# A fused normalise, gate, attention and expert layer: first tile's statistics read from PSUM, its first projection begun with the high parts, the output weights' low parts made earlier

## The chip, the cores and the metric

The kernel runs on one core of one Trainium2 chip. The metric is the device time of one execution in microseconds (us), the median of several runs.

## What is computed

One layer on 8 images of 512 channels by 256 positions, in float32. Cut to what matters:

```
x = x + gate(group_norm(x))                    # per channel a factor from mean, max, std and the MEDIAN of all of them
t = tokens(x)                                  # 8 batches of 256 tokens, 512 wide
t = t + attention(layer_norm(t), w_q, w_k, w_v, w_o)     # 16 heads of 32, tanh softcap, causal mask
t = t + shared_mlp(layer_norm(t)) + top2_of_8_experts(layer_norm(t))
```

layer_norm is (v - mean) / sqrt(var + eps) over the 512 channels of a token.

## The kernel before, in words

Every engine has its own instruction list, written out by hand, and they meet through semaphores only. Names of engines in the profile: PE is TensorE, DVE is VectorE, ACT is ScalarE, POOL is GpSimd, SP issues loads and stores.

**High and low parts.** A float32 matmul operand is split into a high part (rounded by a copy to the type fp32r) and a low part (the operand minus the high part). A product is then three matmuls: high by high, and the two mixed ones. `triple` (line 1566) issues these three for each of the 4 blocks of 128 channels. For the attention weights the split is made in 12 pieces: ACT makes the high piece m (`high_piece`, line 714, writes w_h), POOL the low piece m (`low_piece`, line 534, writes w_l). Pieces 0 to 3 are w_q and w_k (1024 wide each), 4 to 7 are w_v and 8 to 11 are w_o (512 wide each). For the tokens, ACT makes xt_h (`xt_high`, line 743) and DVE xt_l (`xt_low`, line 1188), each in two halves of 256 channels.

**The order of the work.** First the statistics of x and a search for the median in 8 rounds (DVE line 1046 and ACT count half of the values each, PE sums over partitions). In each round ACT also makes one high piece (pieces 4 to 11). Then the lead, on one tile of 256 tokens, and after it steps of attention, one for each batch, in which PE runs the heads of one batch, the projections of the next and the output projection of the one before, all interleaved. The shared MLP and the experts follow.

**The lead** (batch 0) on the engines, in its order:

- DVE `affine(0)` (line 1150) applies the channel factors into `front`.
- PE `y_transposes` (line 1624) turns `front` to tokens, into the PSUM banks YT0 and YT1, 128 tokens each.
- ACT `tokens` (line 737) copies both banks to the SBUF tile T.
- DVE `first_norm` waits until both banks are free again, reads T for the statistics (`tile_stats`, line 1158), joins them (`tile_variance`, lines 1165 and 1167); POOL `rstd_of` (line 549) makes the reciprocal root; DVE `normalised` (line 1173) writes the normalised tile, two instructions, to `front`.
- PE `front_transposes` (line 1635) turns that back to channels, into the banks XN0 and XN1; ACT `xt_high` and DVE `xt_low` split it.
- PE `front_split` waits until XN0 and XN1 are free, that is until both halves of xt_l are made, and then runs the four projections Q0, K0, Q1, K1 (`heads_projection`), 24 matmuls of 256 columns each. Each writes two halves of a bank, 12 matmuls a half.

PE fills two gaps of the lead with dummy matmuls on the identity (`keep_busy`, line 1574; each appears as two passes in the trace). Three PSUM banks (PS5 to PS7, `ring_bank`) are used in turn by all these items; `filled` and `emptied` give the semaphore and the count that say that an item's bank is full or free again (ring_full0 to 2, ring_free0 to 2).

**The first attention step** (batch 0) on PE: scores of head pairs 0 and 1, V's projection, the transposes of the next tile, scores of pairs 2 and 3, then `head_values(0)`, the products of the masked probabilities with V (line 1686). It waits for POOL's masks of pairs 0 and 1 (line 558), for which ACT's exponentials (line 761) must be done, and for both copies of V (ACT line 750). POOL's list here is: low pieces 0 to 7, the root of batch 0, the root of batch 1, low pieces 8 to 11, then the masks of the first step.

Of the kernel before, what the change touches and what calls it, by code (L numbers as in the profile page):

```python
# [17 lines left out]
B, C, S = 8, 512, 256  # L18
# [3 lines left out]
P = 128  # L22
CB = C // P
TT = S // P
# [48 lines left out]
def ring(part, item, b):  # L73

    n = 0
    for name, (steps, items) in PARTS.items():
        if name == part:
            break
        n += steps * len(items)
    n += items.index(item)  # L80
    return n % RING, n // RING + ((b - 1) * (len(items) // RING) if part == "mid" else 0)
# [27 lines left out]
def layer_kernel(nc, x, params, wqkvo, gate, ws, wgu, wd, out):  # L109
    ctx = ExitStack()  # L110
    with ctx:

        def sb(name, shape, dt=fp32, scope=ctx):
            return scope.enter_context(nc.sbuf_tensor(name, shape, dt))
# [42 lines left out]
        w_h = sb("w_h", [P, 4, CB * C], fp32r, scope)  # L157
        w_l = sb("w_l", [P, 4, CB * C], fp32r, scope)
# [24 lines left out]
        bn6 = sb("bn6", [P, TT, 6], fp32, scope)  # L183
# [16 lines left out]
        xt_h = sb("xt_h", [P, CB, S], fp32r, scope)  # L200
        xt_l = sb("xt_l", [P, CB, S], fp32r, scope)
        front = sb("front", [P, CB * S], fp32, scope)
# [104 lines left out]
        score_bank, od_bank, ring_bank = PS[0:4], PS[4], PS[5:8]  # L307
# [7 lines left out]
        def sem(name):  # L315
            return ctx.enter_context(nc.semaphore(name))
# [9 lines left out]
        dve_step, pool_step, act_step = sem("dve_step"), sem("pool_step"), sem("act_step")  # L326
        chmean_ready, grpmean_ready, chvar_ready, grpvar_ready = (
            sem("chmean_ready"), sem("grpmean_ready"), sem("chvar_ready"), sem("grpvar_ready"))
        act_sums = sem("act_sums")
        partial_full, partial_ready = sem("partial_full"), sem("partial_ready")  # L330
        var_ready, root_ready = sem("var_ready"), sem("root_ready")
        u_ready, every_ready, spread_full, uT_full = sem("u_ready"), sem("every_ready"), sem("spread_full"), sem("uT_full")
# [5 lines left out]
        var1_ready, rstd1_ready, var2_ready, rstd2_ready = (  # L338
            sem("var1_ready"), sem("rstd1_ready"), sem("var2_ready"), sem("rstd2_ready"))
        xn_ready, xt_h_done, x2_ready = sem("xn_ready"), sem("xt_h_done"), sem("x2_ready")  # L340
# [49 lines left out]
        def tile_at(b, tt):  # L390

            return at(T, b)[:, tt * C:(tt + 1) * C]

        def filled(part, item, s):

            k, used = ring(part, item, s)
            return ring_full[k], used + 1

        def emptied(part, item, s):

            k, used = ring(part, item, s)
            return ring_free[k], used + 1
# [3 lines left out]
        QK_PIECES, V_PIECES, W_PIECES = 4, 8, 12  # L406

        def piece_of(m, attn):


            if m < QK_PIECES:
                return attn[:, m // 2, 1024 * (m % 2):1024 * (m % 2 + 1)]
            j, k = divmod(m - QK_PIECES, 4)
            return attn[:, 2 + j, 512 * k:512 * (k + 1)]
# [97 lines left out]
        def _(pool):  # L512
# [19 lines left out]
            def low_piece(m):  # L532
                pool.wait_ge(whi_done, m + 1)
                pool.tensor_tensor(piece_of(m, w_l), piece_of(m, w_in), piece_of(m, w_h).bitcast(fp32),
                                   ALU.subtract).then_inc(wlo_done, 1)
# [5 lines left out]


            pool.wait_ge(spread_full, 1)
            for m in range(V_PIECES):
                low_piece(m)

            def rstd_of(var_ready, rstd_ready, b):
                pool.wait_ge(var_ready, b + 1)
                pool.tensor_tensor(rstd[:, :], var_eps[:, :], powers[:, 0:TT], ALU.pow).then_inc(rstd_ready, 1)
# [46 lines left out]
            def step(b, has_next):  # L596
                summed = not (isinstance(b, int) and b == 0)
                for p in range(4):
                    mask(b, p, summed)
                if not (isinstance(b, int) and b == 0):  # L600
                    rstd_of(var2_ready, rstd2_ready, b - 1)
                att_low(b, 0)
                mask(b, 4, summed)
                mask(b, 5, summed)
                att_low(b, 1)
                mask(b, 6, summed)
                mask(b, 7, summed)
                att_low(b, 2)
                att_low(b, 3)
                if has_next:  # L610
                    shared_low(b)
                    rstd_of(var1_ready, rstd1_ready, b + 2)

            rstd_of(var1_ready, rstd1_ready, 0)
            rstd_of(var1_ready, rstd1_ready, 1)
            for m in range(V_PIECES, W_PIECES):
                low_piece(m)
            step(0, True)
            with pool.Fori(1, B - 2) as b:
                step(b, True)  # L620
# [69 lines left out]
        def _(act):  # L690
# [41 lines left out]
            def tokens(part, b, s):  # L732

                for tt in range(TT):
                    act.wait_ge(*filled(part, f"YT{tt}", s))
                    k, _ = ring(part, f"YT{tt}", s)
                    act.activation(tile_at(b, tt), ring_bank[k], ACT.Copy).then_inc(ring_free[k], 1)

# [198 lines left out]
        def _(dve):  # L937
# [207 lines left out]
            def affine(b):  # L1145

                xb = at(T, b).rearrange("p (k s) -> p k s", k=CB)
                ab, bb = coefA[:, bass.ds(b * CB, CB)], coefB[:, bass.ds(b * CB, CB)]
                for k in range(CB):
                    ins = dve.tensor_scalar(front[:, k * S:(k + 1) * S], xb[:, k, :], ab[:, k:k + 1], bb[:, k:k + 1],  # L1150
                                            ALU.mult, ALU.add)
                ins.then_inc(y_ready, 1)

            def tile_stats(b):

                stand_alone(dve)
                for tt in range(TT):
                    step_of(dve.bn_stats(bn6[:, tt, :], tile_at(b, tt)))

            def tile_variance(var_ready):  # L1160

                dve.wait_ge(dve_step, n.value())
                stand_alone(dve)
                for tt in range(TT):
                    step_of(dve.bn_aggr(mean_var[:, tt, :], bn6[:, tt, :]))
                dve.wait_ge(dve_step, n.value())
                dve.tensor_scalar(var_eps[:, :], mean_var[:, :, 1], EPS, None, ALU.add).then_inc(var_ready, 1)

            def normalised(dst, b, rstd_ready):

                dve.wait_ge(rstd_ready, b + 1)
                for tt in range(TT):
                    ins = dve.tensor_scalar(dst[:, tt * C:(tt + 1) * C], tile_at(b, tt), mean_var[:, tt, 0:1],
                                            rstd[:, tt:tt + 1], ALU.subtract, ALU.mult)
                return ins

            def first_norm(part, b, s):
                for tt in range(TT):
                    dve.wait_ge(*emptied(part, f"YT{tt}", s))
                tile_stats(b)  # L1180
                tile_variance(var1_ready)
                normalised(front, b, rstd1_ready).then_inc(xn_ready, 1)
# [130 lines left out]
                gate_top("last", b - 1, b)  # L1313

            affine(0)
            first_norm("lead", 0, 0)
            xt_low("front", 0, 0)
            affine(1)
            for item in ("Q0", "K0", "Q1", "K1"):
# [241 lines left out]
        def _(pe):  # L1561
            def triple(out, parts, lhs, rhs):

                products = [(k, a, b) for k in parts for a, b in ((0, 0), (0, 1), (1, 0))]
                for m, (k, a, b) in enumerate(products):
                    ins = pe.matmul(out, lhs(k, a), rhs(k, b), start=m == 0, stop=m == len(products) - 1)  # L1566
                return ins
# [44 lines left out]
            def begin(part, item, s):  # L1612

                k, used = ring(part, item, s)
                if not (isinstance(used, int) and used == 0):
                    pe.wait_ge(ring_free[k], used)
                return ring_bank[k], ring_full[k]
# [21 lines left out]
            def wslice(t, j, k, lo_, hi_):  # L1639
                return t[:, j, k * C + lo_:k * C + hi_]  # L1640
# [5 lines left out]
            def heads_projection(part, item, s):  # L1646
# [7 lines left out]
                                 lambda k, a: (xt_h, xt_l)[a][:, k, :])  # L1654
                ins.then_inc(full, 1)

            def values_projection(part, s, tt):
                bank, full = begin(part, f"V{tt}", s)
                triple(bank, range(CB), lambda k, a: (xt_h, xt_l)[a][:, k, tt * P:(tt + 1) * P],
                       lambda k, a: wslice((w_h, w_l)[a], 2, k, 0, C)).then_inc(full, 1)  # L1660
# [72 lines left out]
            def front_transposes(part, b, s):  # L1733
                pe.wait_ge(xn_ready, b + 1)
                transposes(part, "XN", front, s)

            def front_split(part, s):
                pe.wait_ge(*emptied(part, "XN0", s))
                pe.wait_ge(*emptied(part, "XN1", s))
# [91 lines left out]
            y_transposes("lead", 0, 0)  # L1831
            keep_busy(16)
            front_transposes("front", 0, 0)
            front_split("front", 0)
            pe.wait_ge(wlo_done, QK_PIECES)
            for item in ("Q0", "K0", "Q1", "K1"):
                heads_projection("front", item, 0)
            y_transposes("front", 1, 0)

# [172 lines left out]
```

## Time and profile before

| | |
|---|---|
| median of 3 runs | 718.38 us (717.37 to 720.6) |
| profiled execution | 718.36 us |
| its span | 716.6 us |
| PE busy | 649.3 us (91%) |
| DVE busy | 443.4 us (62%) |
| ACT busy | 335.8 us (47%) |
| POOL busy | 317.5 us (44%) |

The span is from the first to the last instruction of the profiled execution; its own time is what the runs measure. Busy shares are averages over stages with different limits, so what a change in one stage is worth is read from that stage's waits. In the rows below a line number is that of the kernel before.

### The profile page before, as it was taken

What the parts mean: (1) busy time and instruction counts of PE and PEld (TensorE: products, weight loads), DVE (VectorE), ACT (ScalarE), POOL (GpSimd) and SP (SyncE); (2) the same over time, 40 slices, a digit from 0 to 9 for tenths busy, and PEclk for the clock granted to TensorE, in tenths of its full rate; (3) what the DMA queues carried; (4) which work ended last, traced back from release to release, by engine and by line L of the source; (5) the groups of instructions that cost most, each with busy time, mean ns of one, the idle gap of its engine ahead of it and who ended that gap; (6) DMA issues with size and microseconds to landing.
All of it is one profiled execution on the core that took longest, in us unless ns stands there. A gap on an engine that the chain in (4) does not pass through costs nothing.

```text
span 716.6 us, 14422 instructions
## 1 busy us (share of the span) xinstructions
PE 649.3 (91%) x5030; PEld 553.2 (77%) x5031; DVE 443.4 (62%) x974; ACT 335.8 (47%) x616; POOL 317.5 (44%) x377
## 2 busy tenths in 40 slices
PE   1417989999999999999999999999899999999991
PEld 1407878888888888887789899999677877778771
DVE  7875454757575757573646995223676767667761
ACT  7641364646464646465523123434444454444540
POOL 1340343646464646462421115856345455454534
PEclk9758999999999999999999999999999999999996
DMA  9800000101010101020226323452865555556543
GB/s 307 340 0 1 1 2 1 60 1 59 0 59 0 59 0 59 1 90 1 90 76 240 116 91 113 130 176 70 299 115 96 112 98 107 105 100 111 99 70 44
DMA packets 24787, 62.62 MB, mean 87 GB/s; under 512 B 3056, under 2 KB 7920, under 8 KB 23216
## 3 DMA queue, kind: packets, MB, share of 16 engines
q1 hardware_dynamic: 14912, 41.69, 16.3%
q0 software_dynamic: 9168, 20.45, 15.7%
q8 instruction: 21, 0.34, 0.2%
q10 hardware_dynamic: 672, 0.03, 0.1%
q14 instruction: 14, 0.11, 0.0%
HBM read 39.09 MB, written 23.07 MB: 87 GB/s over the span
## 4 chain that ended last, share of the span: by engine, by line
PE 53%; DMA 27%; DVE 10%; issue 4%; POOL 3%; ACT 1%; DVEq 1%; SPq 0%; POOLq 0%; ACTq 0%
DMA out_tokens<-yo,dest 24%; PE PS L1566 21%; PE scores L1566 12%; PE scores L1858 5%; PE PS L1686 4%; PE scores L1670 3%; PE PS L1635 2%; PE PS L1693 1%; DMA out_tokens<-T 1%; DVE rden L1203 1%; DMA T<-in_x 1%; DVE front L1046 1%; POOL out_tokens L668 1%; PE PS L1624 1%; DVE front L1150 1%
## 5 line engine op out<-in xcount | busy, mean ns | idle before, releaser
L1566 PE MATMUL scores<-xb,sw_h 128*128 128x256 f32 x512 | 94.6, 285 | 0.0
L659 POOL DMA_INDIRECT out_tokens<-yo,dest x36 | 57.1, 1586 | 79.6 <-DMA out_tokens<-yo,dest 77.3
L1566 PEld LDWEIGHTS scores<-xb,sw_h 128*128 128x128 f32 x512 | 81.2, 192 | 2.2 <-ACT probs L757 0.4
L1566 PE MATMUL PS<-xt_h,w_h 128*128 128x256 f32 x256 | 74.5, 291 | 1.6 <-DVE xt_l L1188 1.6
L1566 PE MATMUL scores<-xb,sw_l 128*128 128x256 f32 x256 | 72.5, 283 | 0.0
L1566 PE MATMUL PS<-xt_l,w_h 128*128 128x256 f32 x256 | 72.4, 283 | 0.0
L1566 PE MATMUL PS<-xt_h,w_l 128*128 128x256 f32 x256 | 72.3, 283 | 0.0
L558 POOL TENSOR_SCALAR_AFFINE_SELECT probs<-probs 128x256 f32<-128x256 f32 x128 | 50.4, 418 | 45.6 <-ACT probs L761 45.4
L1566 PE MATMUL scores<-wgu_h,xgT_h 128*128 x156 | 65.0, 417 | 2.1 <-DVE xgT_l L1528 2.1
L1203 DVE RECIPROCAL rden<-PS 128x256 f32<-128x256 f32 x32 | 56.1, 1753 | 13.5 <-PE PS L1686 11.8
L577 POOL TENSOR_TENSOR hl<-hf,hh 128x256 fp32r<-128x256 f32 x32 | 28.5, 890 | 76.3 <-ACT hh L839 76.3
L1566 PE MATMUL scores<-wgu_h,xgT_l 128*128 x156 | 61.1, 391 | 0.0
L907 ACT ACTIVATE wdt_h<-wd_sb 128x512 fp32r x76 | 43.9, 624 | 36.4 <-PE scores L1566 36.4
L1566 PE MATMUL scores<-wgu_l,xgT_h 128*128 x156 | 60.9, 390 | 0.0
L757 ACT ACTIVATE probs<-scores 128x768 f32<-128x768 f32 x64 | 51.3, 802 | 11.2 <-PE scores L1670 11.1
L761 ACT ACTIVATE probs<-probs 128x768 f32<-128x768 f32 x64 | 54.1, 846 | 2.0
L1523 DVE TENSOR_TENSOR wdt_l<-wd_sb,wdt_h 128x512 fp32r<-128x512 f32 x76 | 49.1, 688 | 9.3 <-ACT wdt_h L907 7.6
L1566 PEld LDWEIGHTS PS<-xt_h,w_h 128*128 128x128 f32 x256 | 49.0, 191 | 4.8 <-issue 3.0
L571 POOL TENSOR_TENSOR att_l<-att,att_h 128x256 fp32r<-128x256 f32 x32 | 23.8, 744 | 63.8 <-ACT att_h L765 63.7
L1566 PEld LDWEIGHTS scores<-xb,sw_l 128*128 128x128 f32 x256 | 49.1, 192 | 0.0
L1566 PEld LDWEIGHTS PS<-xt_l,w_h 128*128 128x128 f32 x256 | 49.0, 192 | 0.0
L1566 PEld LDWEIGHTS PS<-xt_h,w_l 128*128 128x128 f32 x256 | 49.0, 192 | 0.0
(304 smaller groups left out, 1623.6 us busy)
## 6 DMA issues: line engine op xcount, KB each, us to landing
wgu_l<-in_wgu SPq DMA_DIRECT2D x8, 1024.0 KB, 7.7
T<-in_x SPq DMA_DIRECT2D x8, 512.0 KB, 7.9
w_in<-in_wqkvo SPq DMA_DIRECT2D x4, 1024.0 KB, 12.1
x_rows<-x SPq DMA_DIRECT2D x8, 512.0 KB, 2.8
x_cols<-x2T SPq DMA_DIRECT2D x8, 512.0 KB, 2.6
xc<-x_cols SPq DMA_DIRECT2D x8, 512.0 KB, 3.9
out_tokens<-T SPq DMA_DIRECT2D x8, 512.0 KB, 7.8
wd_sb<-in_wd SPq DMA_DIRECT2D x8, 512.0 KB, 6.9
```

Of the source, the lines that this page charges most:

```text
L558: ins = pool.affine_select(out=t, in_=t, compare_op=ALU.is_ge, fill=0.0, base=0, pattern=[[0, 2], [1, P]], channel_multiplier=-1)
L571: pool.tensor_tensor(att_l[:, c, :], att[:, :], att_h[:, c, :].bitcast(fp32), ALU.subtract).then_inc(att_l_done, 1)
L577: pool.tensor_tensor(hl[:, j, :], hf[:, j % 2, :], hh[:, j, :].bitcast(fp32), ALU.subtract).then_inc(hl_done, 1)
L659: pool.indirect_dma_start(out[:, :], bass.IndirectOffsetOnAxis(dest[:, t:t + 1], 0), yo[:, t % 3, :], None, compute_op=ALU.add).then_inc(y ...
L757: act.activation(probs[:, p % 4, :].rearrange("p (h q) -> p h q", h=2), scores[:, 2 * (p % 2):2 * (p % 2) + 2, 0:384], ACT.Tanh, scale=1.0 ...
L761: act.activation(probs[:, p % 4, :], probs[:, p % 4, :], ACT.Exp, scale=SOFTCAP).then_inc(exp_done, 1)
L907: act.activation(wdt_h[:, k * C:(k + 1) * C], w[:, k * C:(k + 1) * C], ACT.Copy).then_inc(wdt_h_done, 1)
L1203: dve.wait_ge(dve_step, step_of(dve.reciprocal(rden[:, :], od_bank[:, S:2 * S])))
L1523: dve.tensor_tensor(wdt_l[:, k * C:(k + 1) * C], w[:, k * C:(k + 1) * C], wdt_h[:, k * C:(k + 1) * C].bitcast(fp32), ALU.subtract).then_in ...
L1566: ins = pe.matmul(out, lhs(k, a), rhs(k, b), start=m == 0, stop=m == len(products) - 1)
L1686: ins = pe.matmul(od_bank[j * D:(j + 1) * D, off + tt * P:off + S], lhs(h, tt), pr[:, 0:S] if tt == 0 else pr[:, S:S + P], start=tt == 0, ...
L1858: ins = pe.matmul(dn_bank[tt], (hh, hl)[a][:, j, tt * P:(tt + 1) * P], shared_slice(c, 2, j, 0, C), start=j == 0 and m == 0, stop=j == CB ...
```

## The change

It has three parts. DVE's statistics of the first tile are taken from the two PSUM banks by a new function `lead_norm`; ACT's copies of these banks to T wait for them (semaphore `lead_stats`), so that no two engines read one bank at the same time, and the normalisation waits for the copies. PE's Q0 of the first tile gets a function of its own, `first_projection`: in the first half of the bank it takes the products with xt_h first, and those with xt_l when each half of it is there; the second half of the bank is as before. POOL makes low pieces 8 to 10 straight after piece 7, and piece 11 between the roots of batch 0 and batch 1.

```diff
-            for m in range(V_PIECES):
+            for m in range(W_PIECES - 1):
                 low_piece(m)
...
             rstd_of(var1_ready, rstd1_ready, 0)
+            low_piece(W_PIECES - 1)
             rstd_of(var1_ready, rstd1_ready, 1)
-            for m in range(V_PIECES, W_PIECES):
-                low_piece(m)
             step(0, True)
...
                 for tt in range(TT):
                     act.wait_ge(*filled(part, f"YT{tt}", s))
+                    if part == "lead":
+                        act.wait_ge(lead_stats, tt + 1)
                     k, _ = ring(part, f"YT{tt}", s)
                     act.activation(tile_at(b, tt), ring_bank[k], ACT.Copy).then_inc(ring_free[k], 1)
...
+            def lead_norm():
+
+                for tt in range(TT):
+                    dve.wait_ge(*filled("lead", f"YT{tt}", 0))
+                    k, _ = ring("lead", f"YT{tt}", 0)
+                    dve.bn_stats(bn6[:, tt, :], ring_bank[k]).then_inc(lead_stats, 1)
+                dve.wait_ge(lead_stats, TT)
+                tile_variance(var1_ready)
+                for tt in range(TT):
+                    dve.wait_ge(*emptied("lead", f"YT{tt}", 0))
+                normalised(front, 0, rstd1_ready).then_inc(xn_ready, 1)
...
             affine(0)
-            first_norm("lead", 0, 0)
+            lead_norm()
...
+            def first_projection():
+
+                bank, full = begin("front", "Q0", 0)
+                for h in range(2):
+                    pe.wait_ge(xt_h_done, h + 1)
+                    for k in (2 * h, 2 * h + 1):
+                        pe.matmul(bank[:, 0:S], wslice(w_h, 0, k, 0, P), xt_h[:, k, :], start=k == 0, stop=False)
+                        pe.matmul(bank[:, 0:S], wslice(w_l, 0, k, 0, P), xt_h[:, k, :], start=False, stop=False)
+                for h in range(2):
+                    pe.wait_ge(*emptied("front", f"XN{h}", 0))
+                    for k in (2 * h, 2 * h + 1):
+                        pe.matmul(bank[:, 0:S], wslice(w_h, 0, k, 0, P), xt_l[:, k, :], start=False, stop=k == CB - 1)
+                triple(bank[:, S:2 * S], range(CB), lambda k, a: wslice((w_h, w_l)[a], 0, k, P, 2 * P),
+                       lambda k, a: (xt_h, xt_l)[a][:, k, :]).then_inc(full, 1)
...
             front_transposes("front", 0, 0)
-            front_split("front", 0)
             pe.wait_ge(wlo_done, QK_PIECES)
-            for item in ("Q0", "K0", "Q1", "K1"):
+            first_projection()
+            for item in ("K0", "Q1", "K1"):
                 heads_projection("front", item, 0)
```

How it moves instructions is shown for three engines. On POOL, from the first low piece to the first mask, before:

```order
L534 TENSOR_TENSOR w_l<-w_in,w_h 128x1024 [waits whi_done,spread_full]
L534 TENSOR_TENSOR w_l<-w_in,w_h 128x1024 [waits whi_done] x3
L534 TENSOR_TENSOR w_l<-w_in,w_h 128x512 [waits whi_done] x4
L549 TENSOR_TENSOR rstd<-var_eps,powers 128x2 [waits var1_ready] x2
L534 TENSOR_TENSOR w_l<-w_in,w_h 128x512 [waits whi_done] x4
L558 AFFINE_SELECT probs<-probs 128x2x128 [waits exp_done]
```

and the same place in the changed kernel:

```order
L534 TENSOR_TENSOR w_l<-w_in,w_h 128x1024 [waits whi_done,spread_full]
L534 TENSOR_TENSOR w_l<-w_in,w_h 128x1024 [waits whi_done] x3
L534 TENSOR_TENSOR w_l<-w_in,w_h 128x512 [waits whi_done] x7
L549 TENSOR_TENSOR rstd<-var_eps,powers 128x2 [waits var1_ready]
L534 TENSOR_TENSOR w_l<-w_in,w_h 128x512 [waits whi_done]
L549 TENSOR_TENSOR rstd<-var_eps,powers 128x2 [waits var1_ready]
L558 AFFINE_SELECT probs<-probs 128x2x128 [waits exp_done]
```

Three pieces have moved ahead of the first root, one has come between the two roots, and none is left between the second root and the masks.

On DVE, from the statistics of the first tile to its low parts, before (bn is the statistics, ring_free0 and 1 are the banks YT0 and YT1 free again):

```order
L1158 BN_STATS bn<-T 128x6 [waits ring_free0,ring_free1]
L1158 BN_STATS bn<-T 128x6
L1165 BN_AGGR mean_var<-bn 128x2 [waits dve_step]
L1165 BN_AGGR mean_var<-bn 128x2
L1167 TENSOR_SCALAR var_eps<-mean_var 128x2 [waits dve_step]
L1173 TENSOR_SCALAR front<-T,mean_var,rstd 128x512 [waits rstd1_ready]
L1173 TENSOR_SCALAR front<-T,mean_var,rstd 128x512
```

and in the changed kernel:

```order
L1183 BN_STATS bn<-PS 128x6 [waits ring_full0]
L1183 BN_STATS bn<-PS 128x6 [waits ring_full1]
L1166 BN_AGGR mean_var<-bn 128x2 [waits lead_stats,dve_step]
L1166 BN_AGGR mean_var<-bn 128x2
L1168 TENSOR_SCALAR var_eps<-mean_var 128x2 [waits dve_step]
L1174 TENSOR_SCALAR front<-T,mean_var,rstd 128x512 [waits rstd1_ready,ring_free1,ring_free0]
L1174 TENSOR_SCALAR front<-T,mean_var,rstd 128x512
```

The statistics read PS and wait for a full bank each; the wait for the freed banks has moved down to the normalisation.

On PE, the start of Q0 of the first tile, before (ring_free2 and 0 are XN0 and XN1 free again, ring_free1 is the bank that Q0 writes):

```order
L1566 MATMUL PS<-xt_h,w_h 128x256 [waits wlo_done,ring_free1,ring_free0,ring_free2]
L1566 MATMUL PS<-xt_l,w_h 128x256
L1566 MATMUL PS<-xt_h,w_l 128x256
L1566 MATMUL PS<-xt_h,w_h 128x256
L1566 MATMUL PS<-xt_l,w_h 128x256
L1566 MATMUL PS<-xt_h,w_l 128x256
```

and in the changed kernel, its first half of the bank:

```order
L1676 MATMUL PS<-xt_h,w_h 128x256 [waits xt_h_done,ring_free1,wlo_done]
L1677 MATMUL PS<-xt_h,w_l 128x256
L1676 MATMUL PS<-xt_h,w_h 128x256
L1677 MATMUL PS<-xt_h,w_l 128x256
L1676 MATMUL PS<-xt_h,w_h 128x256 [waits xt_h_done]
L1677 MATMUL PS<-xt_h,w_l 128x256
L1676 MATMUL PS<-xt_h,w_h 128x256
L1677 MATMUL PS<-xt_h,w_l 128x256
L1681 MATMUL PS<-xt_l,w_h 128x256 [waits ring_free2]
L1681 MATMUL PS<-xt_l,w_h 128x256
L1681 MATMUL PS<-xt_l,w_h 128x256 [waits ring_free0]
L1681 MATMUL PS<-xt_l,w_h 128x256
```

The one wait for both halves has become four waits, two for the halves of xt_h and two for those of xt_l.

## Rows read from the trace of the kernel before

**Rows 1.** Page, part 4: the chain that ended last, by engine.

```profile
PE 53%; DMA 27%; DVE 10%; issue 4%; POOL 3%; ACT 1%; DVEq 1%; SPq 0%; POOLq 0%; ACTq 0%
```

**Rows 2.** Windows: length, each engine's busy us, PE clock, DMA share, GB/s.

```profile
55.00:58.00 3.00, 3.00 (x15) 2.98 (x15) 2.19 (x9) 0.23 (x1) 0.00 (x0) 0.50 0.02 5
64.80:68.50 3.70, 1.09 (x8) 0.88 (x9) 2.32 (x5) 1.08 (x2) 0.00 (x0) 1.00 0.01 2
89.60:91.50 1.90, 0.03 (x2) 0.00 (x0) 0.72 (x2) 1.82 (x3) 1.79 (x6) 1.00 0.00 0
91.50:125.00 33.50, 33.46 (x336) 28.38 (x336) 17.47 (x26) 15.88 (x24) 13.74 (x24) 1.00 0.01 2
```

**Rows 3.** Chain in order of time, 57 to 96 us: start, us, what.

```profile
60.78 1.09 ACT T L737 x2
...
62.01 1.30 DVE bn L1158 x2
...
63.98 0.73 POOL rstd L549
...
64.74 1.01 DVE front L1173 x2
...
67.12 0.70 DVE xt_l L1188
...
68.51 11.74 PE PS L1566 x96
...
85.81 4.14 POOL w_l L534 x3
89.95 1.45 POOL probs L558 x4
```

**Rows 4.** Timeline of PE: start, us, instruction; dummy passes, first matmul of K0.

```profile
55.17 4.21 PE L1574 MATMUL scores<-ident 128*128 128x128 f32 x18
61.02 3.74 PE L1574 MATMUL scores<-ident 128*128 128x128 f32 x32
71.45 0.28 PE L1566 MATMUL PS<-xt_h,w_h 128*128 128x256 f32 x1
```

**Rows 5.** Timelines of POOL and DVE: batch 1's root, piece, normalisation; batch 0's normalisation.

```profile
83.91 0.70 POOL L549 TENSOR_TENSOR rstd<-var_eps,powers 128x2 f32<-128x2 f32 x1 [19.21 <-DVE var_eps L1167]
84.57 1.30 POOL L534 TENSOR_TENSOR w_l<-w_in,w_h 128x512 fp32r<-128x512 f32 x1
84.65 1.51 DVE L1173 TENSOR_SCALAR front<-T,mean_var,rstd 128x512 f32<-128x512 f32 x1 [0.81 <-POOL rstd L549]
64.74 0.55 DVE L1173 TENSOR_SCALAR front<-T,mean_var,rstd 128x512 f32<-128x512 f32 x1 [0.84 <-POOL rstd L549]
```

**Rows 6.** Median rounds: durations by line (ns min/median/max), and timelines of POOL, ACT, DVE.

```profile
L534 POOL TENSOR_TENSOR w_l<-w_in,w_h x12: 1266/1384/2347, 29.7 to 88.7; 128x512 fp32r<-128x512 f32 x8, 128x1024 fp32r<-128x1024 f32 x4
L1046 DVE TENSOR_SCALAR_CACHE_REDUCE front<-scores,med x8: 1018/1018/1019, 29.6 to 44.9; 128x768 f32<-128x768 f32 x8
42.55 1.27 POOL L534 TENSOR_TENSOR w_l<-w_in,w_h 128x512 fp32r<-128x512 f32 x1
43.62 0.62 ACT L714 ACTIVATE w_h<-w_in 128x512 fp32r<-128x512 f32 x1
47.48 0.34 DVE L1078 TENSOR_SCALAR_CACHE_REDUCE v<-v,col 96x128 f32<-96x128 f32 x1
```

**Rows 7.** Timelines of ACT, PE and DVE in the first attention step, idle before in brackets.

```profile
84.62 0.85 ACT L761 ACTIVATE probs<-probs 128x768 f32<-128x768 f32 x1
87.91 0.60 ACT L750 ACTIVATE v<-PS 128x512 f32<-128x512 f32 x1 [1.97 <-PE PS L1566]
88.68 0.95 PE L1670 MATMUL scores<-qT,kT 32*128 32x256 f32 x16
89.03 1.29 DVE L1188 TENSOR_TENSOR xt_l<-PS,xt_h 128x512 fp32r<-128x512 f32 x2 [1.45 <-ACT xt_h L743]
91.54 0.86 PE L1686 MATMUL PS<-probs,v 128*32 128x256 f32 x16 [1.91 <-POOL probs L558]
```

More of the change, by code:

```diff
@@ L328, in layer_kernel @@
             sem("chmean_ready"), sem("grpmean_ready"), sem("chvar_ready"), sem("grpvar_ready"))
-        act_sums = sem("act_sums")
+        act_sums, lead_stats = sem("act_sums"), sem("lead_stats")
         partial_full, partial_ready = sem("partial_full"), sem("partial_ready")
```

## The prediction

> **What bounds the kernel now.** Read first the chain that ended last [rows 1]: 53% of it is TensorE, 27% DMA. The DMA part is the expert tail, which can start only when the work ahead of it is done, so time taken out of an early TensorE stretch should arrive at the end whole. Then the windows [rows 2]. Between 91.5 and 125 us TensorE is busy 33.46 of 33.50 us, with a DMA share of 0.01: from there the first attention step is bound by TensorE, and no transfer pins it to a fixed moment. Two stretches before it are not. From 64.8 to 68.5 us TensorE works 1.09 of 3.70 us, and from 89.6 to 91.5 us it works 0.03 of 1.90 us. The change touches what fills both, so I walk the chain there in order of time [rows 3].
>
> In the lead the chain is serial: the transposes of tile 0, ScalarE's two copies to T (60.78, 1.09 us), the two statistics (62.01, 1.30 us), the reciprocal root on GpSimd (63.98), the two normalisations (64.74, 1.01 us), the transposes back and ScalarE's high parts, the low parts (67.12), and only then the first matmul of Q0 (68.51). The second hole ends with GpSimd: its last three pieces of w_o's low parts run from 85.81 to 89.95 us [rows 3], the first masks stand behind them, and the first product with V waits 1.91 us for those masks, starting at 91.54 [rows 7].
>
> **Statistics from PSUM.** VectorE's two statistics no longer wait for the copies; they start when the first bank is full, which is when ScalarE's copy starts now: 60.78, with a pass-on of 0.02 us say 60.80, instead of 62.01 [rows 3]. The second bank is full by the time ScalarE goes on to it, half of 1.09 us later, before one statistic of 0.65 us is done. That is 1.21 us earlier. Reading PSUM is not shown for this operation; the nearest row reads the same 128x512 from PSUM in 1.29 us a pair (the low parts of tile 1) [rows 7], against 1.30 us for the pair of statistics from SBUF, so I price the difference at 0 and keep -0.1 to +0.2 us as its ends. By the Trainium skill's Perfetto Trace Analysis, "Optimizing Scalar/DVE Operations", a VectorE instruction has some 65 ns more overhead on PSUM than on SBUF, which by estimate would be 0.13 us for the two; no run here shows it, and the sum goes without it. The copies to T now stand behind the statistics, but end about 62.7, and the normalisation that reads T starts after 63.5, so they cost nothing; if they did, the normalisation would be late next. The root starts at 63.98 - 1.21 = 62.77, the normalisation could start 0.76 us later, at 63.53, and would be done at 64.54 if nothing stood in its way.
>
> **The last piece in the lead.** Something does. GpSimd now goes from this root straight into piece 11 of w_o. The same meeting is in the trace of before, one tile later [rows 5]: root at 83.91, piece from 84.57 (0.66 us after the root began) to 85.87, and beside it the normalisation, from 84.65. That one took 1.51 us and ended 0.29 us behind the piece, where the undisturbed one of tile 0 took 0.55. So after the change the piece runs from 62.77 + 0.66 = 63.43 to 64.73, the first normalisation ends at 64.73 + 0.29 = 65.02, and the second, with no piece beside it, takes the pair's 1.01 less 0.55 = 0.46 us more: 65.48 against 65.75 before. Of the 1.21 us only **0.27 us** are left. Bounds for the collision: no cost at all (64.54, 0.94 us more gain), or the second also as slow as the first (about 66.5, 1.0 us less).
>
> The Trainium skill's SBUF - State Buffer, "SBUF: two separate sides", speaks against this placement: GpSimd and a VectorE instruction that uses both ports hold the shared ports by an exclusive lock, and whoever comes second fully blocks. Read strictly it would start the first normalisation only at 64.73 and end the pair at 65.74, so that the statistics gain nothing and the total gain is 0.26 us smaller; the row agrees that VectorE waits for the piece, but its 0.29 us behind the piece is shorter than the whole 0.55, and I take the row.
>
> **First projection, high parts first.** Before, Q0's first matmul waits for both halves of the low parts (68.51). Now eight of its first twelve matmuls need only the high parts and the w_l pieces, made long before. The first half of the high parts is done where the low parts start, 67.12 - 0.27 = 66.85; the second half some 0.5 us later, half of what such a pair of copies takes (1.09). The pitch of the projection's matmuls is (71.45 - 68.51) / 24 = 0.1225 us [rows 3, 4]. Four matmuls from 66.9, four more and the two on the first low half from 67.35: ten are issued by 68.1, just before the second low half is there at 68.51 - 0.27 = 68.24. Fourteen remain: 68.24 + 14 x 0.1225 = 69.96, where K0 starts, against 71.45. Gain at this point **1.49 us** (0.27 + 1.22). Bounds: 0 to 1.35 us for this step alone. K0, Q1, K1, the transposes of tile 1 and V's projection are bound by TensorE and move up by the same. VectorE's coefficients for tile 1 run after the low parts, far from being needed.
>
> **Low parts in the median rounds.** Pieces 8 to 10 now follow piece 7, which ends at 42.55 + 1.27 = 43.82 [rows 6]; three times 1.27 us brings GpSimd to at most 47.6. The high part that piece 10 waits for is ready at 43.62 + 0.62 = 44.24, so nothing holds them up, and the root at 62.77 is far away. Do they slow the rounds? In before, the pieces run from 29.7 to 43.8 us and so under seven of the eight rounds, which begin from 29.6 to 44.9 us, and the rounds' long VectorE instruction, which reads PSUM, takes 1018 ns at the least and 1019 ns at the most of eight: no effect. The one instruction they may touch is the count at 47.48, from SBUF to SBUF; I charge **0.05 us**, with 0 and 0.3 as ends.
>
> **The masks.** With one piece in the lead and none behind the second root, GpSimd is free when the exponentials of the first two head pairs are done: 84.62 + 0.85 - 1.49 = 83.98 [rows 7]. Four selects take 1.45 us [rows 3], so both masks are there by 85.5. What is late next is the copy of the second half of V, 87.91 + 0.60 - 1.49 = 87.02, and the scores ahead, 88.68 + 0.95 - 1.49 = 88.14; the latter decides, and the product with V starts there instead of at 91.54. The wait of **1.91 us** is gone. The next wait would be for the low parts of tile 1, 89.03 + 1.29 - 1.49 = 88.83; at least 0.86 us of products lie ahead of it, to 89.0, so it is just covered. The second normalisation also loses its collision, but TensorE's V projection ends after it anyway: 0.
>
> **Sum.** 0.27 + 1.22 - 0.05 + 1.91 = 3.35 us. The profiled execution took 718.36 us (span 716.6, 1.8 around it), which is the median of the runs, 718.38, to 0.02. 718.36 - 3.35 = **715.0 us**. A measurement of this kernel can tell a change from none at about 0.5%, 3.6 us, so the forecast lies just inside "no change", though I think the gain is real.
>
> **Rivals.**
> (a) No collision in the lead: the piece and the normalisation pass each other. Then 0.94 us more, 714.1 us. For it: only one piece is there, not a row of four. Against: the first of the four is the one that cost 0.96 us [rows 5]. Chance 0.10.
> (b) Another wait takes the place of the mask wait: V's copy, the low parts of tile 1 (covered by under 0.2 us), or a slow start of Q0. If all of the 1.91 us comes back, 716.9 us; half of it, 716.0. For it: the thin cover. Against: every one of these is itself moved up by 1.49 us. Chance 0.17.
> (c) The change gains nothing in the end, because the time is lost again before the tail, or because TensorE's order holds the first projection back anyway: 718.4 us. Against: 33.46 of 33.50 us busy right behind it. Chance 0.04.
> (d) Slower: the granted clock falls in the lead. In 55 to 58 us it is 0.50 (1.2 GHz) behind the single small matmuls of the median, and there a dummy pass takes 4.21 / 18 = 0.234 us, against 3.74 / 32 = 0.117 us at full clock [rows 2, 4]. A projection matmul would cost 0.1225 us more, so all 96 of them cost 11.8 us: 726.8 us. It decides from 28 slow matmuls on (3.4 us, the gain), and from 57 it is slower by over 0.5%. For it: the projection now starts in pieces. Against: before, TensorE was busy 1.09 of 3.70 us at a granted 1.00, and the holes get shorter. With it I count the odd surprise of this sign: chance 0.05.
>
> **How the numbers follow.** Forecast 0.64, rivals 0.10, 0.17, 0.04, 0.05. The runs of before spread from 717.37 to 720.6, so about 1 us of noise lies on any median. The line for faster by over 0.5% is 714.8, 0.2 below my forecast: I give four in ten of the forecast's cases (0.26), all of (a) and a little of (b), together 0.38; (d) is slower, 0.05; the rest, 0.57, within 0.5%. The range runs from 713.5 (case (a) with noise) to 717.6 (case (b) in full with noise).
>
> **What would show it right or wrong.** Right: statistics at about 60.8 reading PS; the first normalisation about 1.5 us long, ending behind the one piece; K0's first matmul near 70.0; eleven pieces done by 47.6 with the rounds' instruction still at 1018 ns; no mask wait, the first product with V near 88.1; busy TensorE after it. Wrong: a normalisation pair of 1.0 us (a), a hole of TensorE between 87 and 91 (b), a granted clock below 1.00 after 64 us (d), or a TensorE hole later than 91 that was not there before (c).

## The result, and the profile after

The changed kernel takes 714.36 us (median of 8 runs, 712.8 to 716.03), against 717.68 us for the kernel before over its 8 runs. The ratio is 0.9947, with a 95% interval of 0.9933 to 0.9962. The gain is 3.3 us by the medians and 3.8 us by the ratio; the forecast was 3.35 us. The interval does not reach 1, so the change made the kernel faster, by about half a per cent; on which side of the 0.5% line of the prediction it lies, the interval does not settle.

The profiled execution has a span of 712.4 us, 4.2 less than before. That is more than the change explains, so the lead has to be read by itself. I count times from the first coefficient instruction of tile 0, as the work ahead of it shifts a whole execution (58.66 us before, 59.01 after). In what follows "at 5.0" means 5.0 us behind that instruction.

The chain of waits of the changed kernel, in order of time (start, us, what), answers to [rows 3]:

```profile
59.01 1.39 DVE front L1151 x4
...
61.14 1.31 DVE bn L1183 x2
...
63.15 0.73 POOL rstd L549
...
64.01 1.86 DVE front L1174 x2
...
66.61 0.60 ACT xt_h L744
67.22 0.14 issue
67.35 0.36 PE PS L1676
...
68.55 0.54 PE PS L1681 x4
69.09 10.08 PE PS L1579 x84
...
80.15 0.95 PE scores L1698 x16
...
87.67 0.88 PE scores L1698 x16
88.55 1.44 PE PS L1714 x32
```

The copies to T are gone from the chain, the statistics start at 2.13 (before 3.35) and take 1.31 us, and the first projection matmul follows the first half of the high parts. GpSimd's pieces are gone from the second half: the scores pass straight on to the product with V. The timelines of PE, POOL and DVE show the two places that answer to [rows 5, 7]:

```profile
63.86 1.26 POOL L534 TENSOR_TENSOR w_l<-w_in,w_h 128x512 fp32r<-128x512 f32 x1
64.01 1.39 DVE L1174 TENSOR_SCALAR front<-T,mean_var,rstd 128x512 f32<-128x512 f32 x1 [0.94 <-POOL rstd L549]
88.48 0.86 PE L1714 MATMUL PS<-probs,v 128*32 128x256 f32 x16
```

The normalisation ends at 65.40, 0.28 us behind the piece (65.12). The product with V starts at 29.47, against 32.88 before, with no idle time in front of it: **3.41 us** earlier. The durations by line in the median rounds (ns min/median/max) answer to [rows 6]:

```profile
L534 POOL TENSOR_TENSOR w_l<-w_in,w_h x12: 1253/1263/2345, 30.0 to 63.9; 128x512 fp32r<-128x512 f32 x8, 128x1024 fp32r<-128x1024 f32 x4
L1047 DVE TENSOR_SCALAR_CACHE_REDUCE front<-scores,med x8: 1018/1018/1018, 30.0 to 45.2; 128x768 f32<-128x768 f32 x8
```

and a window behind the product with V to the last one of [rows 2]:

```profile
88.00:121.60 33.60, 33.60 (x349) 28.31 (x342) 18.38 (x28) 17.90 (x26) 13.74 (x24) 1.00 0.01 2
```

The rounds keep their 1018 ns, and TensorE has no hole behind 88 us. Most of the rest of the span's 4.2 us came from the scatter chain at the end, while the later start of the lead took 0.35 us back. That chain begins at 517.37 us before and 514.45 us after (458.71 and 455.44 from the first coefficients, so 3.27 of the 3.41 us arrive there). Its 36 whole scatters then take 1.12 us less. The chain's rows of the kernel before have the first and the last of them at

```profile
517.37 4.86 DMA out_tokens<-yo,dest
...
692.88 4.66 DMA out_tokens<-yo,dest
```

and those of the changed kernel at

```profile
514.45 4.88 DMA out_tokens<-yo,dest
...
688.84 4.53 DMA out_tokens<-yo,dest
```

From the first to the last that is 175.51 us before and 174.39 after. The change does nothing there. Single scatters vary from 4.4 to 5.1 us in both traces, and 36 in a row add up to a microsecond of luck. So a part's effect is read from the lead, and only the sum from the runs.

### The profile page after: what moved, and what is told of

Its sections match the earlier page's. It is cut to its first block, busy times and chain, and to the rows that moved or that the text cites. A ratio compares the mean times of both kernels' runs of the same rounds, so it can differ in the third digit from the quotient of the medians.

```text
span 712.4 us, 14423 instructions
## 1 busy us (share of the span) xinstructions
PE 648.7 (91%) x5030; PEld 552.9 (78%) x5031; DVE 442.1 (62%) x974; ACT 335.5 (47%) x616; POOL 317.2 (45%) x377
## 4 chain that ended last, share of the span: by engine, by line
PE 55%; DMA 27%; DVE 10%; issue 4%; POOL 1%; ACT 1%; DVEq 1%; SPq 0%; POOLq 0%; ACTq 0%
DMA out_tokens<-yo,dest 24%; PE PS L1579 22%; PE scores L1579 12%; PE scores L1886 5%; PE PS L1714 4%; PE scores L1698 4%; PE PS L1648 2%; PE PS L1721 1%; DVE rden L1216 1%; DMA out_tokens<-T 1%; DMA T<-in_x 1%; DMA out_tokens<-yo,dest_halves 1%; DVE front L1047 1%; PE PS L1637 1%; DVE front L1151 1%
## 5 line engine op out<-in xcount | busy, mean ns | idle before, releaser
L1216 DVE RECIPROCAL rden<-PS 128x256 f32<-128x256 f32 x32 | 56.1, 1753 | 11.8 <-PE PS L1714 10.1
L648 POOL DMA_INDIRECT xg<-x_rows,ids x39 | 39.5, 1013 | 19.8 <-issue 10.5
```

Source lines behind the costliest of these rows:

```text
L648: pool.indirect_dma_start(xg[:, t % 3, :], None, x2_rows[:, :], bass.IndirectOffsetOnAxis(ids[:, t:t + 1], 0)).then_inc(xg_loaded[t % 3], 16)
L1216: dve.wait_ge(dve_step, step_of(dve.reciprocal(rden[:, :], od_bank[:, S:2 * S])))
```

## The experiments

They ran on four other chips, on which the kernel before takes 722.4 to 723.5 us, so a time stands only beside the kernel before on the same chip. late_piece ran six times, each other row of the table is one run, and one run says little about its time (proj_only took 720.16 us beside 723.43, 3.27 less, where its marks gain 1.21). So the measured numbers are marks of the trace, counted from the first coefficient instruction. "Transposes" is the start of tile 1's first transposes on TensorE, behind the four projections; "product" is the first product with V.

| kernel | normalisation pair, us | Q0 starts | transposes | product | first projection at 0.50 |
|---|---|---|---|---|---|
| before | 1.00 | 9.85 | 21.43 | 32.88 | no |
| changed | 1.85 | 8.34 | 19.99 | 29.47 | no |
| stats_only | 1.00 | 8.78 | 20.37 | 31.84 | no |
| proj_only | 1.00 | 8.57 | 20.22 | 31.67 | no |
| low_only | 1.94 | 10.79 | 23.77 | 33.24 | yes |
| low_only_again | 1.95 | 11.51 | 24.61 | 34.07 | yes |
| low_warm | 1.95 | 10.81 | 23.88 | 33.36 | yes |
| stats_low | 1.85 | 9.62 | 22.70 | 32.17 | yes |
| stats_low_again | 1.85 | 9.62 | 21.20 | 30.66 | no |
| low_proj | 1.95 | 10.35 | 21.99 | 31.47 | no |
| cool | 1.84 | 8.43 | 21.04 | 30.50 | yes |
| late_piece | 1.00 | 7.50 | 19.14 | 28.69 | no |
| all_in_rounds | 1.00 | 7.49 | 19.13 | 28.59 | no |
| norm_psum | 1.53 | 8.02 | 19.66 | 29.13 | no |

**One part alone.** stats_only is the kernel before with the statistics, ACT's waits and nothing else:

```diff
-            first_norm("lead", 0, 0)
+            lead_norm()
```

> Kernel before with the statistics from PSUM alone; all of w_o's low pieces stay behind the second root. Times are counted from the first coefficient instruction of tile 0 (VectorE, 58.66 us in the trace of before), which takes out the start of the run. My theory (the parts are terms of one serial chain): with no piece beside it the normalisation of tile 0 takes 1.0 us again and ends at 6.0 (before 7.09), so tile 1's first transposes start at 20.35 (before 21.43) and the first product with V at 31.8 (before 32.88): gain 1.1 us. Rival (the copies to T hold the normalisation in place of the statistics): normalisation ends at 7.1, gain 0.

Measured: normalisation from 5.01 to 6.01, transposes at 20.37, product at 31.84. The gain is 1.06 us at the transposes and 1.04 us at the product. ScalarE's copies do not hold the normalisation, so the rival falls.

proj_only:

```diff
-            front_split("front", 0)
             pe.wait_ge(wlo_done, QK_PIECES)
-            for item in ("Q0", "K0", "Q1", "K1"):
+            first_projection()
+            for item in ("K0", "Q1", "K1"):
```

> Kernel before with the first projection's new order alone. My theory: tile 1's first transposes start 1.2 us earlier, at 20.2 after the first coefficients (before 21.43), and the first product with V at 31.7 (before 32.88), still waiting 1.9 us for masks. Rival (the first projection only starts earlier and waits as long inside): transposes at 21.4, gain 0.

Measured: transposes at 20.22, product at 31.67: 1.21 us at both.

low_only:

```diff
-            for m in range(V_PIECES):
+            for m in range(W_PIECES - 1):
                 low_piece(m)
...
             rstd_of(var1_ready, rstd1_ready, 0)
+            low_piece(W_PIECES - 1)
             rstd_of(var1_ready, rstd1_ready, 1)
-            for m in range(V_PIECES, W_PIECES):
-                low_piece(m)
```

> Kernel before with the new places of w_o's low pieces alone. My theory: the mask wait of 1.9 us goes, but the normalisation of tile 0 now meets piece 11 and takes 1.86 us in place of 1.01, so tile 1's first transposes start 0.86 later, at 22.3 after the first coefficients, and the first product with V at 31.8 (before 32.88): net gain 1.1 us. Rival (the collision in the lead is absorbed later, or is no cost): transposes at 21.4, product with V at 30.9, gain 1.9 to 2.0 us.

Measured: the normalisation pair takes 1.94 us and Q0 starts 0.94 us later, where 1.86 and 0.86 were forecast. But the transposes come at 23.77 and the product at 33.24, 0.36 us later than in the kernel before. Neither theory had that. From Q0's start to the transposes it is 12.98 us, against 11.58 before. The timeline of PE shows why, and the window behind it has the granted clock (the third number from the end):

```profile
69.72 0.55 PE L1565 MATMUL PS<-xt_h,w_h 128*128 128x256 f32 x1 [1.62 <-DVE xt_l L1187]
70.07 0.42 PE L1565 MATMUL PS<-xt_l,w_h 128*128 128x256 f32 x1
```

```profile
69.70:72.90 3.20, 3.18 (x15) 3.20 (x16) 1.21 (x4) 0.00 (x0) 0.00 (x0) 0.50 0.00 0
```

The granted clock is 0.50 (1.2 GHz) for the first 15 projection matmuls, which follow each other every 0.21 us in place of 0.12. TensorE had been idle 1.98 us ahead of the second transposes and 1.62 us behind them. This is rival (d) of the prediction, in a part of the change though not in the whole. With the 1.40 us taken off, the product would stand at 31.84, where the theory put it.

**When the clock fell.** low_warm fills the first of these holes, low_only with

```diff
-            keep_busy(16)
+            keep_busy(24)
```

> The low pieces alone, as in low_only, with 24 dummy matmuls in place of 16 ahead of the lead's second transposes, so that TensorE is idle there for about 0.1 us instead of 1.98. Theory (low_only lost 1.4 us because the granted clock fell to 0.50 for the first 15 projection matmuls, after two idle stretches): the clock stays at 1.00, Q0 starts at 10.8 after the first coefficients as in low_only, tile 1's first transposes at 22.3 (low_only 23.77) and the first product with V at 31.8 (33.24). Rival (the slow matmuls have another cause, the pieces or the weights): 23.8 and 33.2 again.

Measured: transposes at 23.88, product at 33.36. These are the rival's numbers, but with a granted clock of 0.50 again: it fell 0.55 us into Q0, although TensorE was idle only 0.20 us ahead of the transposes. So neither my theory of two holes nor the rival's other cause holds. cool goes the other way, from the changed kernel:

```diff
-            keep_busy(16)
+            keep_busy(8)
```

> The changed kernel with 8 dummy matmuls in place of 16 at the same place, so that TensorE is idle for about 2.7 us ahead of the lead's second transposes instead of 0.8. Theory (the changed kernel is spared the fall of the clock only because its idle stretches are short): the granted clock falls to 0.50 somewhere behind the idle stretch and tile 1's first transposes start 1 to 2 us later than the changed kernel's 19.99, at 21 to 22 after the first coefficients. Rival (only the second idle stretch, which the new projection order fills, matters): clock 1.00 and 20.0.

Measured: idle for 2.58 us, then a clock of 0.50 from shortly after the start of the lead's second transposes, which take 1.60 us in place of 1.09, and ten slow matmuls; tile 1's transposes at 21.04, 1.05 us late. The size is as forecast, and the fall came ahead of the second hole, so the rival is out. stats_low is the changed kernel with the old order of Q0 (proj_only's diff undone):

> The changed kernel with the old order of the first projection: statistics from PSUM and the low pieces. Theory (parts add where the clock holds; the statistics bring the transposes forward, so TensorE is idle 0.8 us before them as in the changed kernel): tile 1's first transposes at 21.2 after the first coefficients (19.99 + 1.21), first product with V at 30.7, granted clock 1.00. Rival (the clock falls here as in low_only): 22.6 and 32.1.

Measured: transposes at 22.70, product at 32.17: the rival's numbers. The clock fell at Q0. low_proj is the changed kernel with the old statistics:

```diff
-            lead_norm()
+            first_norm("lead", 0, 0)
```

and without ACT's waits for `lead_stats`.

> The changed kernel with the old statistics: low pieces and the new projection order. TensorE is idle 1.98 us before the second transposes, as in low_only, but only some 0.35 us behind them in place of 1.62. Theory (it takes both idle stretches to make the clock fall): granted clock 1.00, tile 1's first transposes at 21.2 after the first coefficients, first product with V at 30.7. Rival (the first idle stretch alone is enough): clock 0.50 for some matmuls and 22.4 to 22.6.

Measured: no fall at Q0, but here the clock had not yet risen when the lead began. The first transposes took 1.97 us and the dummies ran slow until about 65 us, so that everything stands 0.83 us late from the first normalisation on (6.91 in place of 6.08). Taking that off, the transposes would be at 21.16, as expected. As the dummies ran slow, TensorE was idle only 0.57 us ahead of the second transposes, not the 1.98 that the run was to test, and no clock fell in it. So it doesn't decide between the two holes.

By now two kernels with 1.62 us idle ahead of Q0 had kept the clock (before, stats_only) and three had not (low_only, low_warm, stats_low), with no order between them. So I ran two of them again, unchanged:

> low_only unchanged, executed again. So far the granted clock fell to 0.50 for about 3.4 us at the first projection in low_only, low_warm, stats_low and cool, and not in stats_only and the kernel before, which have the same idle 1.62 us ahead of Q0; the moment when the clock rises ahead of the lead also lies differently in each execution (57.6 to 64.9 us). Theory (when the clock falls in this stretch changes from execution to execution, and the holes only make room for it): the fall is absent or lies elsewhere, and where it is absent tile 1's first transposes start at 22.3 after the first coefficients. Rival (this order of work always makes it fall at Q0): again some 14 slow matmuls from 10.8 and 23.8.

> stats_low unchanged, executed again. Theory (chance from execution to execution): where the clock stays at 1.00, tile 1's first transposes start at 21.2 after the first coefficients and the first product with V at 30.7, which is the sum of the parts. Rival (this order always makes it fall): 15 slow matmuls from 9.6 and 22.7 again.

By the traces the clock rose ahead of the lead at 57.8 us at the earliest (stats_low) and at 64.7 at the latest (low_proj). In low_only it fell again, but earlier, already at the second transposes (Q0 at 11.51, transposes at 24.61). In stats_low it did not: Q0 at 9.62 as in its first execution, transposes at 21.20 and product at 30.66, the sum of the parts to 0.04 us. The same program, the same Q0 start, two clocks, in the window of the first execution and of the second:

```profile
68.00:71.30 3.30, 3.25 (x15) 3.28 (x16) 1.24 (x4) 0.00 (x0) 0.00 (x0) 0.50 0.00 0
```

```profile
69.10:72.00 2.90, 2.87 (x24) 2.90 (x25) 1.21 (x4) 0.00 (x0) 0.00 (x0) 1.00 0.00 0
```

Fifteen matmuls in 3.3 us against 24 in 2.9. So the fall differs between executions of one program, and costs 1.0 to 2.2 us where it comes. What decides it stays open: the two executions ran on different chips, which no run here separates from chance, and in the first the clock had risen 0.64 us ahead of the first coefficients, in the second 1.42 us behind them. The fall was seen only in kernels that had a hole of 1.6 us or more in the lead, and not in every execution of those. The changed kernel has 0.81 us ahead of the second transposes and 0.34 us ahead of Q0, and its one profiled execution kept the clock; whether the short holes make it safe in every execution isn't shown by that one.

**The piece in the lead.** late_piece is the changed kernel with

```diff
             rstd_of(var1_ready, rstd1_ready, 0)
-            low_piece(W_PIECES - 1)
             rstd_of(var1_ready, rstd1_ready, 1)
+            low_piece(W_PIECES - 1)
```

> The changed kernel with piece 11 moved behind the second root, so that the lead has no piece at all. My theory: the normalisation of tile 0 takes 1.0 us in place of 1.86, and tile 1's first transposes start at 19.1 after the first coefficients (changed kernel 19.99), the first product with V at 28.6 (29.47). Piece 11 then collides with the normalisation of tile 1, which has over 1.5 us to spare, and the masks still come 1.5 us early. Gain over the changed kernel 0.85 us, over the kernel before 4.3 us: ratio 0.9940. Rival (the piece only moves the loss to tile 1 or to the masks): product with V at 29.4, ratio as the changed kernel's 0.9947.

Measured over 6 runs: 718.29 us, ratio to the kernel before 0.9926 (0.991 to 0.9943). By the trace the transposes start 0.85 us earlier than in the changed kernel, at 19.14, and the product 0.78 us earlier, at 28.69. The piece now meets the normalisation of tile 1:

```profile
81.84 1.30 POOL L534 TENSOR_TENSOR w_l<-w_in,w_h 128x512 fp32r<-128x512 f32 x1
83.09 1.87 POOL L558 TENSOR_SCALAR_AFFINE_SELECT probs<-probs 128x256 f32<-128x256 f32 x4
81.92 2.05 DVE L1174 TENSOR_SCALAR front<-T,mean_var,rstd 128x512 f32<-128x512 f32 x2 [0.82 <-POOL rstd L549]
86.90 0.86 PE L1714 MATMUL PS<-probs,v 128*32 128x256 f32 x16
```

The masks end at 84.96 and the product starts at 86.90, with 1.9 us to spare. late_piece has a lower ratio than the changed kernel (0.9947), and its trace is 0.8 us ahead; the two ratios come from different chips and their intervals overlap, so the runs alone don't prove it.

all_in_rounds puts piece 11 right behind piece 10:

```diff
-            for m in range(W_PIECES - 1):
+            for m in range(W_PIECES):
...
-            low_piece(W_PIECES - 1)
```

> The changed kernel with all twelve low pieces made in the median rounds; piece 11 then runs for 1.25 us right behind piece 10, from about 0.2 us after the count that follows the rounds has begun. My theory (a VectorE instruction that finds GpSimd in a piece waits for that piece's end, when it works from SBUF to SBUF; the rounds escape because they read PSUM): the lead is as without a piece, normalisation 1.0 us, but the five VectorE instructions behind the rounds meet piece 11 and are done about 0.5 to 1.2 us later. The stretch from the last round's end to the first coefficients grows by that, and the net against the changed kernel lies between -0.35 and +0.35 us. Rival (small instructions of 96x128 do not feel GpSimd): that stretch keeps its length and the kernel gains 0.85 us.

Measured: the lead is free (product at 28.59), but the stretch from the last round's count to the first coefficients is 14.55 us in place of 13.76, 0.79 longer. One instruction makes it up, as the timelines of POOL and DVE show:

```profile
46.53 2.50 POOL L534 TENSOR_TENSOR w_l<-w_in,w_h 128x512 fp32r<-128x512 f32 x2
47.79 0.34 DVE L1078 TENSOR_SCALAR_CACHE_REDUCE v<-v,col 96x128 f32<-96x128 f32 x1
48.06 1.06 DVE L1065 TENSOR_SCALAR v<-v,col 96x128 f32<-96x128 f32 x1
```

and in the kernel before, where no piece runs there:

```profile
47.75 0.28 DVE L1065 TENSOR_SCALAR v<-v,col 96x128 f32<-96x128 f32 x1
```

The last two pieces end at 49.03, and the TENSOR_SCALAR ends at 49.12. The count ahead of it keeps its 0.34 us, though it too runs from SBUF to SBUF beside the piece. So my rule "from SBUF to SBUF" was too wide. The net against the changed kernel is -0.09 us at the product (0.79 - 0.88), within the range expected.

norm_psum keeps piece 11 in the lead and lets the normalisation read PSUM:

```diff
-                normalised(front, 0, rstd1_ready).then_inc(xn_ready, 1)
+                dve.wait_ge(rstd1_ready, 1)
+                for tt in range(TT):
+                    k, _ = ring("lead", f"YT{tt}", 0)
+                    ins = dve.tensor_scalar(front[:, tt * C:(tt + 1) * C], ring_bank[k], mean_var[:, tt, 0:1],
+                                            rstd[:, tt:tt + 1], ALU.subtract, ALU.mult)
+                ins.then_inc(xn_ready, 1)
```

> The changed kernel, piece 11 still in the lead, but tile 0's two normalisations read the PSUM banks in place of T. My theory (only instructions from SBUF to SBUF wait for the piece): they run beside the piece at 0.65 us each, the pair takes 1.3 us in place of 1.85, and tile 1's first transposes start 0.55 us earlier, at 19.45 after the first coefficients. Rival A (any VectorE instruction beside a piece is held, whatever it reads): pair 1.85 to 2.0 us, no gain. Rival B (reading PSUM costs nothing extra): pair 1.0 us, gain 0.85.

Measured: 1.53 us for the pair, between my 1.3 and rival A's 1.85. The two instructions one by one, and the piece:

```profile
63.20 1.26 POOL L534 TENSOR_TENSOR w_l<-w_in,w_h 128x512 fp32r<-128x512 f32 x1
63.35 0.81 DVE L1191 TENSOR_SCALAR front<-PS,mean_var,rstd 128x512 f32<-128x512 f32 x1 [0.94 <-POOL rstd L549]
64.08 0.80 DVE L1191 TENSOR_SCALAR front<-PS,mean_var,rstd 128x512 f32<-128x512 f32 x1
```

The first runs wholly beside the piece (63.20 to 64.46) and is done before it, so a normalisation that reads PSUM isn't held until the piece's end. The second runs beside it for 0.38 of its 0.80 us and takes as long as the first. So the extra over 0.55 us is likely the price of PSUM for this instruction and not of the piece; a run without any piece beside it was not made.

## Why the prediction was right

**Statistics from PSUM.** Forecast 1.21 us to the root, measured 1.18 (4.14 from the first coefficients, before 5.32). The pair takes 1.31 us against 1.30 from SBUF, so the price of 0 was right. The 0.13 us estimated from the Trainium skill's Perfetto Trace Analysis, "Optimizing Scalar/DVE Operations", does not show for this operation. What the prediction missed is 0.10 us behind the root: the normalisation starts 0.86 us after the root's start, where it was 0.76 before, so only 1.08 us of the gain arrive there (stats_only: 1.06 at the transposes). The copies are not the reason, as they end at 4.11, ahead of the root; two more waits stand in front of the instruction, but no run shows that they are the cause.

**The last piece in the lead.** Forecast: the first normalisation ends 0.29 us behind the piece, the pair takes 1.95 us and leaves 0.27 us of the gain. Measured 0.28, 1.86 and 0.23 us (the pair ends at 6.86, before 7.09). late_piece puts the price of the collision at 0.85 us, where the prediction had 0.94, and rival (a) is refuted. The sum does not feel the 0.10 us that both terms miss, because the end of the pair follows the piece's end, and so the root, whenever the normalisation started. On the Trainium skill's SBUF — State Buffer, "SBUF: two separate sides", by which whichever comes second fully blocks: the traces agree that a held VectorE instruction ends only behind the piece, and that only some VectorE instructions are held. The count with an accumulator (0.34 us beside a piece) and the PSUM reads (0.81 and 0.80) aren't. A strict reading, 0.55 us from the piece's end, is too long by 0.27 us: 0.28, 0.29 and 0.09 us are what was left at the piece's end in the changed kernel, in low_only and in all_in_rounds. Whether the instruction stands still until then or creeps, these rows don't tell.

**First projection.** Forecast 1.22 us, measured 1.21 both alone (proj_only) and beside the other parts (21.20 in stats_low_again less 19.99).

**Median rounds.** Nothing was lost: the rounds keep 1018 ns, and the stretch behind them is 13.76 us against 13.77. The 0.05 us charged was not needed. The count does not meet a piece (piece 10 ends at 47.83, where the count starts), and all_in_rounds shows that it would not have waited. The instruction behind it would have: it starts 0.27 us after the piece's end, so this term was safe by that much only.

**The masks.** Forecast 1.91 us, measured 1.97 (3.41 at the product less 1.44 at the transposes). The low parts of tile 1 were covered, so rival (b) did not come.

**The sum** of these is 3.41 us where the prediction had 3.40 before the 0.05. It arrived at the scatter chain within 0.14 us, so rival (c) fell. That the medians also differ by 3.32 us is partly luck, as the 95% interval of the ratio spans some 2 us. The forecast time of 715.0 us lies 0.6 above the measured median, because it started from 718.36 and the kernel before took 717.68 in its eight runs. Rival (d) did not happen in the profiled execution, but it was closer than its 0.05 suggests. The low pieces without the other two parts met it in both executions of low_only and in low_warm, and its price in a part is 1.0 to 2.2 us, far from the 11.8 us that I reckoned for a clock that stays low. The prediction treated the parts as terms that add; they do add (20.37, 20.22 and 21.20 all fit), but only while the clock holds.

## What to carry to other kernels

Before moving background work on GpSimd into a gap, look at which VectorE instruction stands next on the critical chain. One that is held for the length of a piece gives back most of what was won, and the same piece one root later was free. When a lead is worked on in parts, judge each by marks of its own stretch and look at the granted clock first: a part can lose more at 1.2 GHz than it gains, as low_only did, and a single trace doesn't tell whether it will in the next execution.

## What the runs showed of the hardware that was not expected

- Two executions of one program on two chips, with Q0 starting at 9.62 us in both, were granted 0.50 and 1.00 for it, which puts tile 1's transposes 1.50 us apart. In low_proj the clock had not risen at the start of the lead, where in late_piece it had.
- A normalising TENSOR_SCALAR of 128x512 takes 0.80 us from PSUM, with a piece beside it, and 0.55 us from SBUF with none, while the statistics take the same from both (1.31 and 1.30 us a pair).
- Beside a GpSimd piece a TENSOR_SCALAR from SBUF to SBUF of 96x128 took 1.06 us in place of 0.28, and the count of the same size with an accumulator output kept 0.34.
